# Expert stage: ids and two-part weights turned on TensorE in float16, maxima by a reduction, a reordered second layer

## The reference

```python
h = layernorm(x) * (1 + ca) + sa
# layer 0 attention: 8 heads, rank 64, values of width 128
Q, K, V = (h @ Wq.T), (h @ Wk.T), (h @ Wv.T)
x = x + ga * einsum(softmax(Q K^T), V)            # 1024 x 1024 scores per head, summed over heads
h = layernorm(x) * (1 + cb) + sb
# layer 0 experts (product keys): batch norm of h @ w_q over all tokens, then per token and head
sx, ix = top_k(sim[0], 8); sy, iy = top_k(sim[1], 8)         # of 32 keys each
scores, pk = top_k(sx[:, None] + sy[None, :], 8)             # of the 64 sums
indices = ix * 32 + iy at pk                                  # of 1024 experts
hid = gelu(x . down_embed[indices]) * softmax(scores)
x = x + gb * sum(hid * up_embed[indices])
# layer 1 attention: unit norm, three projections, a gated scan over the 1024 tokens
q, kv, a = split(h / |h| * sqrt(128) * gamma @ W_qkva.T); y = scan(sigmoid(a), kv); x = x + ga * q * y
# layer 1 feed-forward: mixes of each token with the one before, r = sigmoid(.), k = relu(.)^2
x = x + gb * r * (k @ W_v.T)
```

## Time and profile before

| | |
|---|---|
| median of 3 runs | 2973.26 us (2972.37 to 2979.75) |
| profiled execution | 2971.47 us, span 2969.7 us |
| attention | from the start to about 1800 us |
| tables | about 1800 to 1867 us |
| experts | about 1867 to 2748 us |
| second layer | about 2749 us to the end |
| busy over the span | PE 2745.0, DVE 2262.9, ACT 2180.5, POOL 1766.1 us |
| mean granted TensorE clock | 0.914 |

### The profile page before, as it was taken

How to read it: one execution, slowest core, us unless ns; L and a number is a source line. 1 busy time by engine, 2 the same in 40 slices (tenths; PEclk the granted TensorE clock), 3 DMA queues, 4 the chain that set the end, 5 groups by cost and what they waited for, 6 DMA issues and landing times. The chain is left out here.

```text
span 2969.7 us, 77592 instructions
## 1 busy us (share of the span) xinstructions
PE 2745.0 (92%) x27940; PEld 2073.0 (70%) x27940; DVE 2262.9 (76%) x8471; ACT 2180.5 (73%) x4273; POOL 1766.1 (59%) x1756
## 2 busy tenths in 40 slices
PE   5999999999999999999999996699999999998688
PEld 3777777777777777777777775467666766666343
DVE  5676776776776776776767756799999999996564
ACT  3888887888888888888888881366766667665675
POOL 3788888788887888888778782233333333331111
PEclk7999999999999999999999997678877878877798
DMA  3000000000000000000000001100000000000000
GB/s 106 1 1 8 1 1 8 1 1 8 1 1 8 1 1 8 1 1 8 1 1 8 1 1 65 68 0 0 0 0 0 0 0 0 0 0 2 8 22 29
DMA packets 11793, 27.63 MB, mean 9 GB/s; under 512 B 1529, under 2 KB 6137, under 8 KB 11137
## 3 DMA queue, kind: packets, MB, share of 16 engines
q1 hardware_dynamic: 11618, 25.48, 2.5%
HBM read 17.07 MB, written 8.40 MB: 9 GB/s over the span
## 5 line engine op out<-in xcount | busy, mean ns | idle before, releaser
L284 POOL TENSOR_TENSOR probs_l<-probs,probs_h 128x512 fp32r<-128x512 f32 x1024 | 1302.5, 1294 | 325.2 <-ACT probs_h L378 321.3
L377 ACT ACTIVATE probs<-bank 128x512 f32<-128x512 f32 x1024 | 638.4, 623 | 278.2 <-PE bank L698 194.1
L539 DVE TENSOR_REDUCE maxes<-ring 128x1 f32<-128x512 f32 x1024 | 659.5, 686 | 183.3 <-PE ring L678 182.2
L378 ACT ACTIVATE probs_h<-bank 128x512 fp32r<-128x512 f32 x1024 | 640.4, 625 | 0.0
L697 PE MATMUL bank<-q_hh,k_hl 128*128 128x512 f32 x1024 | 424.7, 415 | 2.4 <-ACT probs_h L378 2.2
L698 PE MATMUL bank<-q_lm,k_h 65*128 65x512 f32 x1024 | 405.9, 396 | 0.0
L708 PE MATMUL obank<-probs_h,x_l 128*128 128x512 f32 x1024 | 405.2, 396 | 0.0
L710 PE MATMUL obank<-probs_h,x_h 128*128 128x512 f32 x1024 | 403.8, 394 | 0.0
L709 PE MATMUL obank<-probs_l,x_h 128*128 128x512 f32 x1024 | 403.1, 394 | 0.0
L678 PE MATMUL ring<-k_hl,q_hh 128*128 128x512 f32 x1024 | 339.5, 412 | 12.0 <-DVE maxes L539 7.3
L1074 ACT ACTIVATE low_hot<-obank 128x512 f16<-128x512 f32 x512 | 296.9, 604 | 56.9 <-PE obank L1249 43.5
(11 more groups left out here) (252 smaller groups left out, 4865.2 us busy)
## 6 DMA issues: line engine op xcount, KB each, us to landing
xt<-in_x SPq DMA_DIRECT2D x8, 512.0 KB, 9.8
out_x<-xt SPq DMA_DIRECT2D x8, 512.0 KB, 2.6
x<-out_x SPq DMA_DIRECT2D x1, 4096.0 KB, 12.1
out_x<-x SPq DMA_DIRECT2D x16, 256.0 KB, 2.1
mod<-out_x SPq DMA_DIRECT2D x3, 512.0 KB, 13.6
pk_wq<-in_w_q SPq DMA_DIRECT2D x1, 1024.0 KB, 4.9
pk_wqT<-in_w_qT SPq DMA_DIRECT2D x1, 1024.0 KB, 7.0
hot_rule<-in_hot_rule SPq DMA_DIRECT2D x1, 776.0 KB
```

What stands on the lines that cost most here:

```text
L284: nc.gpsimd.tensor_tensor(probs_l[:, i, :], probs[:, s % 4, :], probs_h[:, i, :].bitcast(F32), ALU.subtract).then_inc(low_ready, 1)
L377: nc.scalar.activation(probs[:, s % 4, :], st[s % 4], ACT.Exp)
L378: nc.scalar.activation(probs_h[:, i, :], st[s % 4], ACT.Exp).then_inc(st_free[s % 4], 1)
L539: nc.vector.tensor_reduce(maxes[:, i, k:k + 1], ring[bank_of(at)][:], AX.X, ALU.max).then_inc(rows_maxed, 1)
```

## The change

- Attention: the two maxima of a row are joined by a reduction over one tensor and not by a maximum of two. Parts 5 to 8 of `second_norm` move from head 1 to head 2 of the next batch; 3 and 4 stay in head 1, one at each of steps 13 and 14.
- Experts: the ids are cast to float16 and not to float32; the shares are split into a coarse (ScalarE, new `coarse_shares`) and a fine part (VectorE, last of `front`) before they are turned; TensorE turns four 128x128 tiles with float16 matmuls by an identity; ScalarE reads both parts out of the bank. VectorE's instruction on the bank (1190) is gone. The subtraction of the maximum moves to GpSimd (`less_best`), between the candidates and the slots.
- Second layer: first moments and `normed` are made two batches ahead, with two buffers for `l_h`; `mix_normed` moves from ScalarE to VectorE, to the head of the next iteration, and needs no shift; TensorE's projections of the first half come before the turn of `l_mixed`; the variance comes before the floor of the norm.

```diff
-                nc.vector.tensor_tensor(row_max[:], maxes[:, :, 0], maxes[:, :, 1], ALU.max).then_inc(max_ready, 1)
+                nc.vector.tensor_reduce(row_max[:], maxes[:], AX.X, ALU.max).then_inc(max_ready, 1)
...
-                        if h == 1 and s >= 13 and not first:
-                            for n in range(2 * (s - 13) + 3, 2 * (s - 13) + 5):
+                        if h == 1 and s in (13, 14) and not first:
+                            second_norm(link, s - 10, b - 1)
+                        if h == 2 and s in (13, 14) and not first:
+                            for n in range(2 * (s - 13) + 5, 2 * (s - 13) + 7):
                                 second_norm(link, n, b - 1)
...
-        to_turn = sb("to_turn", [P, 3, P])
+        to_turn = sb("to_turn", [P, 4, P], F16)
+        shares = sb("shares", [P, P])
+        ident_h = sb("ident_h", [P, P], F16)
...
+            def coarse_shares(u):
+                act.wait_ge(shares_ready, u + 1)
+                nc.scalar.activation(to_turn[:, 2, :], shares[:], ACT.Copy, scale=W_SCALE).then_inc(coarse_share, 1)
+
             def turned_ids(u):
...
-                nc.scalar.activation(parts[:, 0], spread(turn_bank[:, 256:384], 2, 2), ACT.Copy, scale=W_SCALE).then_inc(coarse_ready, 1)
+                nc.scalar.activation(parts[:, 0], spread(turn_bank[:, 256:384], 2, 2), ACT.Copy).then_inc(parts_ready, 1)
+                nc.scalar.activation(parts[:, 1], spread(turn_bank[:, 384:512], 2, 2), ACT.Copy).then_inc(parts_ready, 1)
...
             exponentials(0)
+            coarse_shares(0)
             front(1)
             split_ids(0)
             turned_ids(0)
...
                 exponentials(u + 1)
                 centred(u + 2)
+                coarse_shares(u + 1)
                 split_ids(u + 1)
...
-                link(last)
-                nc.vector.tensor_tensor(expd[:], best[:], spread(best[:, :, 0], 2, TOPK), ALU.subtract).then_inc(less_max, 1)
+                last.then_inc(best_ready, 1)
+                dve.wait_ge(best_ready, u + 1)
...
+                dve.wait_ge(coarse_share, u + 1)
+                nc.vector.scalar_tensor_tensor(to_turn[:, 3, :], shares[:], W_SCALE, to_turn[:, 2, :], ALU.mult, ALU.subtract).then_inc(weights_ready, 1)
...
-                dve.wait_ge(coarse_ready, u + 1)
-                nc.vector.scalar_tensor_tensor(parts[:, 1], spread(turn_bank[:, 256:384], 2, 2), W_SCALE, parts[:, 0], ALU.mult, ALU.subtract).then_inc(fine_ready, 1)
-                dve.wait_ge(fine_ready, u + 1)
+                dve.wait_ge(parts_ready, 2 * u + 2)
...
-                for s in range(3):
-                    mm = nc.tensor.transpose(turn_bank[:, s * P:(s + 1) * P], to_turn[:, s, :], ident[:])
+                for s in range(4):
+                    mm = nc.tensor.matmul(turn_bank[:, s * P:(s + 1) * P], to_turn[:, s, :], ident_h[:], start=True, stop=True)
...
+            def less_best(u):
+                pool.wait_ge(best_ready, u + 1)
+                nc.gpsimd.sem_inc(turns, 1)
+                nc.gpsimd.tensor_tensor(expd[:], best[:], spread(best[:, :, 0], 2, TOPK), ALU.subtract).then_inc(less_max, 1)
...
                 if b + 1 < B:
-                    first_rstd(b + 1)
                     norm_root(b + 1)
                 second_rstd(b)
...
+            def mix_normed(b):
+                dve.wait_ge(rstd2_ready, b + 1)
                 if b:
-                    dve.wait_ge(mixed_ready, 2 * b)
-                moments_of(1, b)
...
+                    dve.wait_ge(mix_turned, 2 * b)
+                for t in range(TB):
+                    made = nc.vector.tensor_scalar(mixed[:, t], x2[:, b * TB + t], mean_var[:, 1, t, 0:1], rstd[:, 1, t:t + 1], ALU.subtract, ALU.mult)
+                    if t % 4 == 3:
+                        made.then_inc(mixed_ready, 1)
...
             for b in range(B + 1):
-                scanning, mixing, ahead = b < B, b > 0, b + 1 < B
-                if ahead:
-                    first_moments(b + 1)
-                    first_shift(b + 1)
+                scanning, mixing = b < B, b > 0
+                if mixing:
+                    mix_normed(b - 1)
+                if b + 2 < B:
+                    first_moments(b + 2)
...
                     second_moments(b)
-                if ahead:
+                    variance_of(1, var2_ready)
+                if b + 1 < B:
                     floor_norm(b + 1)
-                if scanning:
-                    variance_of(1, var2_ready)
...
                 if scanning:
                     turn_units(b)
+                    scan_products(b, 0)
                 if mixing:
                     turn_mixed(b - 1)
                 if scanning:
-                    scan_products(b, 0)
                     scan_products(b, 1)
```

More of the change, by code:

```diff
@@ L993, in build_experts @@
         less_max = sem("ex_less_max")
+        best_ready = sem("ex_best")
+        shares_ready = sem("ex_shares")
+        coarse_share = sem("ex_coarse_share")
+        ident_ready = sem("ex_ident")
         exp_done = sem("ex_exp")
@@ L1385, in _ @@
             candidates(0)
+            less_best(0)
             slots(0)
@@ L1437, in build_second_layer @@
         r_norm = sb("l1_r_norm", [P, TB])
-        h = sb("l1_h", [P, TB, D])
+        h = [sb(f"l1_h{i}", [P, TB, D]) for i in range(2)]
         unit = sb("l1_unit", [P, TB, D])
@@ L1560, in sums_of_squares @@
                 for t in range(TB):
-                    last = nc.scalar.activation(unit[:, t], h[:, t], ACT.Square, accum_out=squares[:, t:t + 1])
+                    last = nc.scalar.activation(unit[:, t], h[b % 2][:, t], ACT.Square, accum_out=squares[:, t:t + 1])
                 last.then_inc(squares_ready, 1)
@@ L1566, in unit_rows @@
                 for t in range(TB):
-                    made = nc.scalar.activation(unit[:, t], h[:, t], ACT.Copy, scale=r_norm[:, t:t + 1])
+                    made = nc.scalar.activation(unit[:, t], h[b % 2][:, t], ACT.Copy, scale=r_norm[:, t:t + 1])
                     if t % 4 == 3:
@@ L1578, in decays @@
                 nc.scalar.activation(decay[:, half(k)], ring[k][:], ACT.Sigmoid).then_inc(decay_ready, 1)
-            def mix_normed(b):
-                act.wait_ge(shift2_ready, b + 1)
-                for t in range(TB):
-                    made = nc.scalar.activation(mixed[:, t], x2[:, b * TB + t], ACT.Identity, bias=shift[:, 1, t:t + 1], scale=rstd[:, 1, t:t + 1])
-                    if t % 4 == 3:
-                        made.then_inc(mixed_ready, 1)
             def shifted_h(b):
@@ L1624, in _ @@
                     gates(b - 1, 1)
-                if ahead:
+                if b + 1 < B:
                     unit_rows(b + 1)
-                if scanning:
-                    mix_normed(b)
         @block.vector
@@ L1658, in first_shift @@
                 dve.wait_ge(rstd1_ready, b + 1)
[L1659 removed]
+                nc.vector.scalar_tensor_tensor(shift[:], mean_var[:, 0, :, 0], -1.0, rstd[:, 0], ALU.mult, ALU.mult).then_inc(shift1_ready, 1)
             def scaled(b):
                 dve.wait_ge(normed_ready, b + 1)
[L1663 removed]
+                link(nc.vector.scalar_tensor_tensor(h[b % 2][:], row(1, b), 1.0, h[b % 2][:], ALU.add, ALU.mult))
             def moved(b):
[L1666 removed]
+                nc.vector.tensor_tensor(h[b % 2][:], h[b % 2][:], row(0, b), ALU.add).then_inc(h_ready, 1)
             def floor_norm(b):
```

56 lines of the change are left out of this document (29 added, 27 removed).

## The result

The changed kernel took 2927.68 us in the median of 4 runs (2926.95 to 2930.16), the kernel before 2976.51 us on the same chip: ratio 0.9827, 95% interval 0.9806 to 0.9849. Forecast were 2929 us. The profiled executions have spans of 2969.7 and 2925.2 us, so 44.5 us less, where the forecast was 43.9.

| stretch | before | after | forecast of the change |
|---|---|---|---|
| first to last turn of `wv_gated` (line 669), 63 heads | 1719.4 | 1696.3 | -22.8 |
| copy of `w_eff` to `low_hot` of unit 0 | 26.0 | 31.0 | +4.5 |
| `low_hot` of unit 0 to that of unit 31 | 823.4 | 810.8 | -14.6 |
| start of the second layer to the second add of batch 0 | 30.9 | 35.1 | 0 |
| second add of batch 0 to that of batch 7 | 163.3 | 144.3 | -10.8 |

A forecast was written before the change was run, and what follows sets the result against it. Bounds: TensorE in attention, VectorE in the expert loop, a chain across engines in the second layer. Terms 22.8 + 14.6 - 4.5 + 11 = 43.9 us gained gave 2929 us against 2973.3; 8-in-10 range 2913 to 2948.

The forecast's parts named there:

- What bounds each stage: Whole kernel: TensorE limits attention, VectorE the expert loop, a chain across engines the second layer.
- Row maxima, 9.6 us: Attention: the reduction takes 0.2 us and never queues, so two long heads gain 4.78 us each; at worst nothing.
- Norms moved, 13.2 us: Attention: moving 3.6 us of norms to head 2 ends the late key split, 1.88 us in 7 batches.
- the late split: Attention, end of head 1: VectorE's key split starts only after the norms, costing TensorE 1.88 us.
- Expert loop, 0.47 us per unit: Expert loop, VectorE: subtraction 0.21, bank instruction 0.33, `low_hot` 0.15 gained, product-minus 0.22 lost; 14.6 us over 31 distances.
- Before the loop, 4.5 us lost: Before the expert loop: unit 0's coarse cast delays unit 1's centred copy on ScalarE; 4.5 us lost once, bounds 2 and 5.5.
- Second layer, 10.8 us in the batches: Second layer: the chain from unit rows to first projection shortens by 1.5 us per batch, 10.8 us over 7 distances.
- the upper bound: Second layer: 17 us gained if TensorE's shorter pauses leave it more at the full clock.
- Its start, 0 net: Second layer's start: the second batch's norm moves ahead, about 1 us lost on ScalarE, 1 regained in batch 0.
- the five: Rivals: reduction queues, 0.09; VectorE awaits coarse cast, 0.12; second layer unmoved, 0.13; two together, 0.04; TensorE bounds loop, 0.02.
- Rival 2: Expert loop: VectorE waits 0.3 to 0.5 us for the coarse cast in each unit; about 2943 us; chance 0.12.
- its worst ends: Whole kernel: the worst ends of all parts together were said to give 2972 us.

The follow-up runs named there:

- the mended order: Changed kernel with unit 0's coarse cast after unit 1's copies and batch 0 scaled before batch 1's moments: 2921.76 us; again 2918.86 against the changed kernel's 2923.88.

## Why the prediction was right, and where not

- **What bounds each stage.** Right. All gains came where the windows had put the limit, and the parts alone add up to the whole within what their intervals can tell.
- **Row maxima, 9.6 us.** The mechanism was right (no maximum over 171 ns), and so was the price of 4.78 us for a held one. But the step counted the held maxima of one execution, and their number is a matter of chance. In the profile the term came out as forecast; in the medians it is about 15 us (the reduction alone, 15.5). The 48.8 us between the medians, against 43.9 forecast, owe 4 to 5 us to this.
- **Norms moved, 13.2 us.** Right: seven heads of 28.37 us are at 26.5, alone and together. The four instructions took 5.6 us in head 2 in place of 3.6, and 1.2 us of room was left. The case that the prediction feared, GpSimd blocking each of them, came in part: three of four are some 0.9 us longer than the 0.7 us without it, in place of one. And the late split in head 1 was itself such a price: with GpSimd's instructions halved it is gone.
- **Expert loop, 0.47 us per unit.** Measured 0.49 without the edges. The sum is right by errors that cancel: the subtraction gave 0.06 to 0.15 (forecast 0.21), since the wait for the last MAX8 came out from under it; the bank instruction gave 0.43 (0.33), since `value_hot` now follows with no hand-over; the new product-minus cost 0.20 (0.22); `low_hot` gave 0.13 (0.15), by the step forecast; `z` gave 0.06, not forecast. From the first to the last `low_hot` the loop gained 12.6 us and not 14.6, since the distances at its two edges grew by 1.7 us; they differ by some us between executions. GpSimd needs 0.40 us for what VectorE did in 0.29, and nobody waits for it. By the Trainium skill (GPSIMD Engine Reference, "4.1 Engine selection") it would be twice as slow; the row has 1.4 times, and the row decides.
- **Before the loop, 4.5 us lost.** Measured 5.0, by the step forecast: the coarse cast waited 5.44 us for the shares, with the centred copy behind it in ScalarE's queue. That the mended order gives back 1.3 us only was not seen.
- **Second layer, 10.8 us in the batches.** The term was mis-sized: 19.0 us. The step of the chain was right, 1.46 us a batch against 1.5. What had been left at the upper bound ("if TensorE's shorter pauses leave it more at the full clock") is what happened: another 1.7 us in six of seven distances. The 21.96 us between two adds of the kernel before, with its projections at 1.12 us, was there to be read and would have given it.
- **Its start, 0 net.** Mis-sized too: 4.1 and 4.2 us lost in the two profiles of the changed kernel, 2.5 and 2.7 in two others with the same second layer, where the clock rose earlier. Forecast was 1 us lost on ScalarE and 1 regained. In fact VectorE's moments of batch 1 wait for `normed(0)` and then for GpSimd's power, with the scaling of batch 0 behind them, and ScalarE's normalisation of batch 1 takes 3.19 us ahead of the squares of batch 0:

```profile
2728.96 1.64 DVE L1657 BATCH_NORM_STATS2 l_moments<-x 128x6 f32<-128x128 f32 x8 [2.18 <-ACT l_h L1580]
2733.23 0.17 DVE L1674 SCALAR_TENSOR_TENSOR l_shift<-l_mean_var,l_rstd 128x8 f32<-128x8 f32 x1 [1.75 <-POOL l_rstd L1545]
```

```profile
2733.44 3.19 ACT L1580 ACTIVATE l_h<-x,l_shift,l_rstd 128x128 f32<-128x128 f32 x8 [2.66 <-DVE l_shift L1674]
```

  The mended order has 3.1 to 3.4 us less than the changed kernel's profiles, and 1.5 to 1.8 less than those two others.
- **Rivals.** None of the five came. Rival 2 shows up in one place: in the first unit of the loop VectorE waits 3.79 us for the coarse cast, which stands behind `hcT`, and `hcT` behind TensorE. In the other units it doesn't wait. One sum of the prediction is off without consequence: its worst ends add up to 3.5 us gained, which is 2970 and not 2972.

So the steps were right, but that the total came within 1 us is luck: the clock's gain (about +8), the lost start (-4), the loop's edges (-2) and some 1 us in the rest of the span nearly cancelled, and the number of held maxima moves the kernel before by more than that.

## What to carry to other kernels

An instruction whose median is several times its shortest at constant work is waiting inside itself: look at what the engine that shares its port does at that time, and count the cases over more than one execution before pricing them. Where TensorE's products run at two speeds at the same place of a repeated piece, the difference between those repetitions is the price of the clock, and filling the pauses ahead can win it where they come back in each repetition; ahead of the first one here it was gone by the next batch. When a piece of work is moved ahead in the start of a pipeline, write down what stands behind it in each queue: both places where this change lost were such. And before a gain of 1 or 2 us is read from one profile, look at the same stretch in another kernel that has the same code there.

## What was not expected of the hardware

- A 128x8 maximum of 0.16 us was held for 5.17 us behind GpSimd instructions that follow each other without a pause, and in other batches from one execution to the next; the time of the kernel before spreads over 30 us, that of the changed kernel over 2 to 3 us, but for one execution of 3993 us.
- The other way, a GpSimd copy of 0.28 us was held for 4.44 us by one VectorE instruction of 4.42 us; whether it starts 0.1 us before or after that one moved the first unit of the loop by 4 us.
- Twelve transposes that nobody reads, in pauses of 0.5 to 0.9 us, took 1.7 us off a batch of 23.65 us.
